# A stream of gated cross-attention layers: bias row as a TensorE product, norms shared, adds and setup moved

## The chip, the cores and the metric

The kernel runs on one core of one Trainium2 chip. The metric is the device time of one execution in microseconds (us), lower is better. A core has five engines that run their own instruction streams and meet at semaphores: TensorE (PE, with its weight loads PEld), VectorE (DVE), ScalarE (ACT), GpSimd (POOL) and SyncE (SP, which issues DMAs). All data is float32.

## What is computed

Four decoder layers work on x, 16 sequences of 256 rows and 128 features. Each adds a gated cross-attention over 64 context rows (16 heads of 8), then a gated feed-forward part; a layer norm precedes each.

```python
x = x + tanh(g_xattn[l]) * xattn_l(layernorm(x), ctx)   # softmax(q k' / sqrt(8) + bias_l) v, then @ Wo.T + bo
x = x + tanh(g_ffn[l])   * ffn_l(layernorm(x))
# ffn_0: 8 experts, 2 chosen a row, and a shared expert;  ffn_1: x @ (ternary weights).T
# ffn_2: 4 experts with fixed gates, relu;                ffn_3: 8 experts, 1 chosen a row
```

## The kernel before

The program has these stages on each engine, in this order: layer norm and attention of layer 0 (to about 249 us), the router's logits, ranks (`rank_tensor`, `route_vector`), the shared expert (`shared_*`), a setup, the experts of layer 0 (`moe_*`), then the **stream** (about 590 to 1141 us), and after it norm, routing and experts of layer 3.

The setup (`tern_prepare_vector`, `setup_tensor`, `setup_vector`) rounds the ternary weights and computes, for layers 1 to 3, the row `bvc @ Wo + bo` (value bias through the output projection, plus the output bias). `setup_tensor` makes that row on all 128 partitions of bank psM and begins with a wait for `s_tw`, which DVE's first instruction of `tern_prepare_vector` (L1166) raises. `setup_vector` multiplies it by the layer's gate into `bx` (L1193). DVE's order is `route_vector`, `shared_vector`, `tern_prepare_vector`, `setup_vector`, `moe_vector`; PE's is `rank_tensor`, `shared_tensor`, `setup_tensor`, `moe_tensor`.

The stream is a software pipeline over 48 batches (16 in each of the layers 1, 2, 3), written out by hand: step n, from -5 to 49, does for several batches one part each, in a fixed order on each engine.

- PE: turns probabilities (L1325, four times), queries of batch n+3 (L1301), values weighed (L1340, twice), heads turned (L1357), outputs turned (L1347), the transposes of a norm (`norm_rows`, L1294), an expert's first product (`four_up`, L1381), then keys, values (L1286), the ternary product (L1370) or the expert's second product (`four_down`, L1389), the projection of batch n-2 (L1363), and last the scores of batch n+3 (L1314).
- ACT: copies each of these out of PSUM (L1453, L1459, L1465, L1471, L1479), takes exponentials (L1475) and the experts' relus (L1486). The last two relus must end before the step's scores, which write the same banks.
- DVE: adds the mask bias (L1536, two tiles), row maxima (L1544, two tiles), between these the ternary result (`add_ternary`, L1574) or an expert's result (`add_four`, L1583) that PE made in the step before, scales the outputs of batch n-1 (L1549, L1553), and adds the projection of batch n-2 to x with row statistics (`add_attention`, L1561).
- POOL: subtracts the maxima (`shift`, L1620, two tiles), computes scale and shift of a norm from the statistics (`spread`, L1628 to L1638, seven small instructions), normalises 4 tiles of 128 rows (a chunk; L1647) and adds a bias row to x (`add_row`, L1654): `bx` after the norm for the queries, so that the attention's bias is already in x, and `b2c` after that for the experts of layer 2.

Query norms run at odd n on POOL and are transposed by PE at n+1; feed-forward norms run at even n and are transposed at n+1. One PSUM bank, psB, is shared: norm transposes, keys, values, the ternary product and the experts' second product fill it in turn. `take_bank` waits until its last user has read it (`s_free`); for the ternary and expert products that is DVE's add, one step later. The 16 first products of layer 2's experts lie on steps 22 to 29, 31 to 37 and 39 (`up_step`), each second product one step behind. Steps are counted in the text by their scores: those of step n are the last products that PE makes in it.

Of the kernel before, what the change touches and what calls it, by code (L numbers as in the profile page):

```python
# [21 lines left out]
P = 128  # L22
# [70 lines left out]
def build(nc, ins, out, sorted_x, sorted_y):  # L93
    ctx = ExitStack()
    with ctx:
# [19 lines left out]
        bx = sb("bx", [P, LAYERS - 1, D])  # L115
# [92 lines left out]
        lna = sb("lna", [P, CH, 2])  # L208
        lnd = sb("lnd", [P, CH])
        lnr = sb("lnr", [P, CH])  # L210
        lnh = sb("lnh", [P, CH])
# [36 lines left out]
        s_bx, s_b2 = sem("attention_bias_added"), sem("expert_bias_added")  # L248
# [978 lines left out]
        def values_at(n):  # L1227

            return {2: (2, 0), 3: (2, 1), 4: (2, 2), 5: (2, 3), 17: (3, 0), 19: (3, 1), 21: (3, 2), 22: (3, 3)}.get(n)
# [18 lines left out]
        for n in range(FIRST, FINAL):  # L1248
            for kind, c in (("query", query_norm(n - 1)), ("ffn", ffn_norm(n - 1))):
# [21 lines left out]
        def stream_tensor(pe):  # L1271
# [125 lines left out]
            for n in range(FIRST, FINAL):  # L1397
# [14 lines left out]
                if ffn_norm(n - 1) is not None:  # L1412
                    norm_rows(("ffn", ffn_norm(n - 1)))
# [21 lines left out]
        def stream_scalar(act):  # L1435
# [57 lines left out]
            for n in range(FIRST, FINAL):  # L1493
# [14 lines left out]
                if ffn_norm(n - 1) is not None:  # L1508
                    keep_normed(("ffn", ffn_norm(n - 1)))
# [17 lines left out]
        def stream_vector(dve):  # L1527
# [65 lines left out]
            for n in range(FIRST, FINAL):  # L1593
# [4 lines left out]
                if ternary_at(n - 1) is not None:  # L1598
                    add_ternary(ternary_at(n - 1))
                if down_at(n - 1) is not None:  # L1600
                    add_four(down_at(n - 1))
                if 0 <= 2 * n + 5 < NU:
                    row_max(2 * n + 5)
                if 0 <= n - 1 < NB:
                    scale_outputs(n - 1)
                if 0 <= n - 2 < NB:
                    add_attention(n - 2)

        def stream_gpsimd(pool):
# [12 lines left out]
            def spread(use):  # L1622

                c = use[1]
                if normed[use]:
                    pool.wait_ge(s_xn, normed[use])
                tiles = slice(c % NC * CH, c % NC * CH + CH)
                step(nc.gpsimd.tensor_tensor(lna[:], st[:, tiles, 1:3], st[:, tiles, 4:6], ALU.add))  # L1628
                step(nc.gpsimd.tensor_tensor(lnd[:], st[:, tiles, 1], st[:, tiles, 4], ALU.subtract))
                pool.wait_ge(s_lnp, steps[0])  # L1630
                step(nc.gpsimd.tensor_tensor(lna[:], lna[:], lnc[:].rearrange("p c -> p () c").broadcast_to([P, CH, 2]), ALU.mult))
                step(nc.gpsimd.tensor_tensor(lnd[:], lnd[:], lnd[:], ALU.mult))
                pool.wait_ge(s_lnp, steps[0])
                step(nc.gpsimd.tensor_scalar(lnd[:], lnd[:], 0.25, EPS, ALU.mult, ALU.add))
                pool.wait_ge(s_lnp, steps[0])
                step(nc.gpsimd.tensor_tensor(lnd[:], lnd[:], lna[:, :, 1], ALU.add))
                pool.wait_ge(s_lnp, steps[0])
                step(nc.gpsimd.tensor_tensor(lnr[:], lnd[:], lnh[:], ALU.pow))  # L1638

            def normalise(use):  # L1640
                kind, c = use
                m = normed[use]
                if m > 1:
                    pool.wait_ge(s_full, turn[[k for k in normed if normed[k] == m - 2][0]] + 1)
# [163 lines left out]
```

## Time and profile before

| | |
|---|---|
| median of 3 runs | 1357.03 us (1356.96 to 1357.54) |
| the profiled execution | 1357.12 us, its span 1355.2 us |
| busy over the span | PE 1055.8, DVE 781.6, ACT 659.0, POOL 698.0 us |
| stream, 623 to 728 us (105 us) | PE 91.6, DVE 77.6, ACT 73.7, POOL 92.3 us |
| stream, 728 to 820 us (92 us) | PE 78.7, DVE 68.6, ACT 64.4, POOL 82.7 us |
| stream, 820 to 940 us (120 us) | PE 103.1, DVE 56.9, ACT 66.9, POOL 69.0 us |
| stream, 940 to 1085 us (145 us) | PE 126.7, DVE 71.7, ACT 78.6, POOL 79.9 us |
| chain that ended last | PE 57%, DVE 13%, issue 11%, ACT 8%, POOL 7% |
| granted PE clock | 0.90 on the mean; 1.0 in most of the stream; 0.5 (1.2 GHz) at 280 to 292 us, 370 to 385 us and 1147 to 1184 us |

The profile gives for each instruction its engine, its line in the kernel, what it writes and reads, its start and duration, and what ended the idle time ahead of it. Busy time alone doesn't say what bounds a stage, since each engine also waits for the others inside a step. The timeline of a step shows that: who starts the moment that whose work ends.

### The profile page before, as it was taken

What the parts mean: (1) busy time and instruction counts of PE and PEld (TensorE: products, weight loads), DVE (VectorE), ACT (ScalarE), POOL (GpSimd) and SP (SyncE); (2) the same over time, 40 slices, a digit from 0 to 9 for tenths busy, and PEclk for the clock granted to TensorE, in tenths of its full rate; (3) what the DMA queues carried; (4) which work ended last, traced back from release to release, by engine and by line L of the source; (5) the groups of instructions that cost most, each with busy time, mean ns of one, the idle gap of its engine ahead of it and who ended that gap; (6) DMA issues with size and microseconds to landing.
All of it is one profiled execution on the core that took longest, in us unless ns stands there. A gap on an engine that the chain in (4) does not pass through costs nothing.

```text
span 1355.2 us, 26685 instructions
## 1 busy us (share of the span) xinstructions
PE 1055.8 (78%) x9100; PEld 852.9 (63%) x9100; DVE 781.6 (58%) x1697; ACT 659.0 (49%) x1372; POOL 698.0 (52%) x900
## 2 busy tenths in 40 slices
PE   0699999669979999547988889888888886508990
PEld 0477776446779999425766666666566664408990
DVE  3899998350076665555787775445544585234652
ACT  1544443333145666227767765545555565205650
POOL 0254454117781071676999897555654451055224
PEclk9799999669978999558999999999999998558995
DMA  8900000001121242100000000000400000002323
GB/s 252 285 6 1 1 1 1 1 4 47 61 69 47 77 114 73 51 19 1 2 1 1 2 2 1 1 1 2 140 1 1 1 2 1 0 31 90 89 72 93
DMA packets 75428, 55.81 MB, mean 41 GB/s; under 512 B 7363, under 2 KB 68419, under 8 KB 75204
## 3 DMA queue, kind: packets, MB, share of 16 engines
q1 hardware_dynamic: 69188, 41.92, 10.8%
q0 software_dynamic: 6144, 12.60, 3.1%
q8 instruction: 62, 1.02, 0.3%
q14 instruction: 34, 0.28, 0.1%
HBM read 32.48 MB, written 22.02 MB: 40 GB/s over the span
## 4 chain that ended last, share of the span: by engine, by line
PE 57%; DVE 13%; issue 11%; ACT 8%; POOL 7%; SPq 1%; DMA 1%; DVEq 1%; ACTq 0%; POOLq 0%
PE psS L966 9%; PE psO L972 8%; PE psO L1389 4%; PE psS L1381 4%; PE psS L1314 3%; PE psT L1325 3%; POOL xrows L1137 3%; PE psO L895 2%; PE psS L887 2%; PE psM L461 2%; PE psO L1340 2%; DVE rden L679 2%; DVE mx L1544 2%; ACT xrows L1486 2%; DVE ring L667 2%
## 5 line engine op out<-in xcount | busy, mean ns | idle before, releaser
L1620 POOL TENSOR_TENSOR ring<-ring,mx 128x1024 f32<-128x1024 f32 x96 | 182.3, 1903 | 145.8 <-DVE mx L1544 145.6
L1453 ACT ACTIVATE pT<-psT 128x512 f32<-128x512 f32 x192 | 114.8, 598 | 157.9 <-PE psT L1325 157.4
L1017 ACT ACTIVATE pT<-psS,b1copy 128x128 f32<-128x128 f32 x512 | 145.9, 368 | 87.4 <-PE psS L966 87.4
L1137 POOL DMA_INDIRECT xrows<-sorted_y,rows x96 | 92.4, 962 | 182.8 <-DMA sorted_y<-pT 95.1
L966 PE MATMUL psS<-ring 128*128 128x128 f32 x1024 | 140.4, 282 | 12.3 <-DVE ring L1040 11.6
L1536 DVE TENSOR_TENSOR ring<-psS,bias 128x1024 f32<-128x1024 f32 x96 | 113.1, 1220 | 61.9 <-PE psS L1314 61.8
L972 PE MATMUL psO<-ring,pT 128*128 128x128 f32 x1024 | 137.5, 278 | 0.7 <-ACT pT L1017 0.7
L966 PEld LDWEIGHTS psS<-ring 128*128 128x128 f32 x1024 | 129.4, 199 | 13.2 <-issue 7.9
L1325 PE MATMUL psT<-ident,ring 128*128 128x128 f32 x768 | 123.0, 283 | 15.0 <-ACT pT L1453 14.2
L741 POOL TENSOR_TENSOR ring<-ring,rden 128x1024 f32<-128x1024 f32 x32 | 75.3, 2354 | 114.6 <-DVE rden L681 114.6
L972 PEld LDWEIGHTS psO<-ring,pT 128*128 128x128 f32 x1024 | 126.8, 195 | 1.1 <-ACT pT L1017 1.1
L1325 PEld LDWEIGHTS psT<-ident,ring 128*128 128x128 f32 x768 | 86.0, 143 | 57.0 <-issue 34.5
L1037 DVE COPY ring<-w 128x512 f32 x128 | 60.2, 470 | 95.3 <-PE psO L972 73.5
L1544 DVE TENSOR_REDUCE mx<-ring 128x16 f32<-128x1024 f32 x96 | 114.0, 1208 | 0.0
L1125 POOL DMA_INDIRECT sorted_x<-late,ix x96 | 93.7, 976 | 37.0 <-issue 24.1
L1561 DVE SCALAR_TENSOR_TENSOR x<-psM,tg,x 128x256 f32<-128x256 f32 x48 | 23.2, 483 | 145.5 <-PE psM L1363 145.4
L1475 ACT ACTIVATE ring<-ring 128x1024 f32<-128x1024 f32 x96 | 101.5, 1059 | 0.0
L629 ACT ACTIVATE pT<-psT 128x512 f32<-128x512 f32 x64 | 38.2, 597 | 75.5 <-PE psT L545 75.5
L1647 POOL TENSOR_SCALAR xn<-x,lna,lnr 128x128 f32<-128x128 f32 x160 | 69.7, 450 | 0.2
L1294 PE MATMUL psO<-ident,xn 128*128 128x128 f32 x160 | 26.3, 290 | 55.7 <-POOL xn L1647 27.6
L679 DVE TENSOR_REDUCE rden<-ring 128x64 f32<-128x1024 f32 x32 | 61.4, 1917 | 0.0
L1389 PE MATMUL psO<-w,xrows 128*128 128x128 f32 x512 | 60.0, 276 | 1.5 <-ACT kblk L1479 0.8
(229 smaller groups left out, 2227.4 us busy)
## 6 DMA issues: line engine op xcount, KB each, us to landing
w<-w_dram SPq DMA_DIRECT2D x34, 256.0 KB, 6.0
ring<-sorted_x SPq DMA_DIRECT2D x32, 256.0 KB, 2.9
sorted_y<-pT SPq DMA_DIRECT2D x32, 256.0 KB, 2.3
sorted_x<-late SPq DMA_DIRECT2D x20, 256.0 KB, 3.5
out_dram<-x SPq DMA_DIRECT2D x1, 2048.0 KB, 8.7
sorted_x<-late,ix POOLq DMA_INDIRECT x96, 2.2
xrows<-sorted_y,rows POOLq DMA_INDIRECT x96
ctxz<-ctxz_dram SPq DMA_DIRECT2D x1, 1056.0 KB, 11.9
```

The source lines that it names most:

```text
L966: mm = nc.tensor.matmul(psS[:, t % 2, f * P:(f + 1) * P], wcopy[:, t, 0, f, :], xgT[:, s, t * P:(t + 1) * P], start=True, stop=True)
L972: mm = nc.tensor.matmul(psO[:, s, t * P:(t + 1) * P], hs[:, t % 2, f, :], wcopy[:, t, 1, f, :], start=(f == 0), stop=(f == nf - 1))
L1017: op = nc.scalar.activation(hs[:, t % 2, f, :], psS[:, t % 2, f * P:(f + 1) * P], func, bias=b1copy[:, t, f:f + 1])
L1125: nc.gpsimd.indirect_dma_start(sorted_x[h], bass.IndirectOffsetOnAxis(ix[:, s, m:m + 1], 0), xstage[:, s, m // nch, :], None).then_inc(s_s ...
L1137: nc.gpsimd.indirect_dma_start(fetched[:, at + m, :], None, sorted_y[c // (NC // 2)], bass.IndirectOffsetOnAxis(rows[:, c * nt + m:c * nt ...
L1325: mm = nc.tensor.transpose(psT[:, i * P:(i + 1) * P], ring[:, u % NS, p * P:(p + 1) * P], ident[:])
L1389: mm = nc.tensor.matmul(psB[:, t * P:(t + 1) * P], fourT[:, i % 2, k, t * P:(t + 1) * P], w22[:, e, f, :], start=(k == 0), stop=(k == 3))
L1453: nc.scalar.activation(pT[:, u % 2, 4 * h:4 * h + 4, :].rearrange("p a q -> p (a q)"), psT[:, :], ACT.Copy).then_inc(s_pT, 1)
L1475: nc.scalar.activation(ring[:, u % NS, :], ring[:, u % NS, :], ACT.Exp).then_inc(s_exp, 1)
L1536: nc.vector.tensor_tensor(ring[:, u % NS, :].rearrange("p (g h k) -> p g h k", g=NG, h=GH), psS[:, :, qt * 256:(qt + 1) * 256].rearrange(" ...
L1544: nc.vector.tensor_reduce(mx[:, u % 4, 0:NH], ring[:, u % NS, :].rearrange("p (h k) -> p h k", k=SK), AXX, ALU.max).then_inc(s_max, 1)
L1620: nc.gpsimd.tensor_tensor(rows_, rows_, mx[:, u % 4, 0:NH].rearrange("p h -> p h ()").broadcast_to([P, NH, SK]), ALU.subtract).then_inc(s_ ...
```

## The change

Five things are changed together.

1. The gate is left out of the bias row. `bx` is gone; `bo` holds the row for each layer, and PE adds it to the projection by a one-row product (ones times row) accumulated behind each of the two products of L1363. `add_row` is no longer called for the queries, and `add_attention` no longer waits for it.
2. The feed-forward norms run at odd n, with the query norms, and `spread` does the small instructions once for both, over two chunks. The feed-forward chunk is normalised one step later (even n) and transposed by PE at odd n; the ternary product moves from step 2c+6 to 2c+8.
3. `add_ternary` and `add_four` run on DVE in the step in which PE makes the product, after the outputs are scaled, not in the next step between the row maxima.
4. The experts' first products lie on steps 24 to 39 without a gap; one value product moves from step 22 to 23.
5. The setup runs ahead of the shared expert, on PE and on DVE.

```diff
-                nc.vector.tensor_scalar(bx[:, l - 1, :], psM[:, l * D:(l + 1) * D], tg[:, l:l + 1], None, ALU.mult).then_inc(s_four, 1)
+                nc.vector.tensor_copy(bo[:, l, :], psM[0:1, l * D:(l + 1) * D]).then_inc(s_four, 1)
...
         def ffn_norm(n):
-            return (n - 4) // 2 if n % 2 == 0 and 0 <= (n - 4) // 2 < 2 * B // 2 else None
+            return (n - 5) // 2 if n % 2 and 0 <= (n - 5) // 2 < 2 * B // 2 else None
...
         def ternary_at(n):
-            return (n - 6) // 2 if n % 2 == 0 and 0 <= (n - 6) // 2 < B // 2 else None
-        up_step = [22 + 17 * i // 15 for i in range(2 * NC)]
+            return (n - 8) // 2 if n % 2 == 0 and 0 <= (n - 8) // 2 < B // 2 else None
+        up_step = [24 + i for i in range(2 * NC)]
...
             def project(n):
                 pe.wait_ge(s_onT, n + 1)
                 for qt in range(QT):
-                    mm = nc.tensor.matmul(psY[:, qt * P:(qt + 1) * P], onT[:, qt * P:(qt + 1) * P], wat[:, layer(n), 3, :], start=True, stop=True)
+                    nc.tensor.matmul(psY[:, qt * P:(qt + 1) * P], onT[:, qt * P:(qt + 1) * P], wat[:, layer(n), 3, :], start=True, stop=False)
+                    mm = nc.tensor.matmul(psY[:, qt * P:(qt + 1) * P], ones1[:, :], bo[:, layer(n), :], start=False, stop=True)
                 mm.then_inc(s_y, 1)
...
-                if ffn_norm(n - 1) is not None:
-                    norm_rows(("ffn", ffn_norm(n - 1)))
+                if ffn_norm(n - 2) is not None:
+                    norm_rows(("ffn", ffn_norm(n - 2)))
...
                 dve.wait_ge(s_y, n + 1)
-                dve.wait_ge(s_bx, n // 2 + 1)
...
-                if ternary_at(n - 1) is not None:
-                    add_ternary(ternary_at(n - 1))
-                if down_at(n - 1) is not None:
-                    add_four(down_at(n - 1))
                 if 0 <= 2 * n + 5 < NU:
                     row_max(2 * n + 5)
                 if 0 <= n - 1 < NB:
                     scale_outputs(n - 1)
+                if ternary_at(n) is not None:
+                    add_ternary(ternary_at(n))
+                if down_at(n) is not None:
+                    add_four(down_at(n))
                 if 0 <= n - 2 < NB:
                     add_attention(n - 2)
...
-                cq, cf = query_norm(n), ffn_norm(n)
+                cq, cf, last = query_norm(n), ffn_norm(n), ffn_norm(n - 1)
...
-                    spread(("query", cq))
                 if cf is not None:
                     pool.wait_ge(s_bnf, CH * (cf + 1))
-                    spread(("ffn", cf))
+                if cq is not None or cf is not None:
+                    spread(cq, cf)
                 if 0 <= 2 * n + 5 < NU:
                     shift(2 * n + 5)
                 if cq is not None:
                     normalise(("query", cq))
-                    add_row(("query", cq), bx[:, layer(2 * cq) - 1, :], s_bx)
-                if cf is not None:
-                    normalise(("ffn", cf))
-                    if cf >= B // 2:
-                        add_row(("ffn", cf), b2c[:], s_b2)
+                if last is not None:
+                    normalise(("ffn", last))
+                    if last >= B // 2:
+                        add_row(("ffn", last), b2c[:], s_b2)
...
             rank_tensor(pe, 0)
+            setup_tensor(pe)
             shared_tensor(pe)
-            setup_tensor(pe)
...
             route_vector(dve, 0)
-            shared_vector(dve)
             tern_prepare_vector(dve)
             setup_vector(dve)
+            shared_vector(dve)
```

## Rows read from the trace of the kernel before

**Rows 1.** Waits of PE: who <- whom, us in all, times, longest us.

```profile
PE psO L1294 <- DVE x L1583: 17.1, 13, 1.3
...
PE psO L1294 <- DVE x L1574: 11.0, 8, 1.4
```

**Rows 2.** Timeline: start, duration (us), engine, line, tiles [idle <- releaser]; late steps.

```profile
1062.11 1.15 PE L1314 MATMUL psS<-xnT,qTs 32*128 32x256 f32 x16
...
1084.68 1.15 PE L1314 MATMUL psS<-xnT,qTs 32*128 32x256 f32 x16
...
1093.44 1.15 PE L1314 MATMUL psS<-xnT,qTs 32*128 32x256 f32 x16
...
1101.26 1.15 PE L1314 MATMUL psS<-xnT,qTs 32*128 32x256 f32 x16
...
1108.59 1.15 PE L1314 MATMUL psS<-xnT,qTs 32*128 32x256 f32 x16
```

**Rows 3.** Timeline: plain products, then the shared expert's with one-row products.

```profile
535.20 1.06 PE L966 MATMUL psS<-ring 128*128 128x128 f32 x8
...
536.09 1.05 PE L972 MATMUL psO<-ring,pT 128*128 128x128 f32 x8
...
311.08 1.16 PE L895 MATMUL psO<-w,ring 128*128 128x128 f32 x8
...
312.17 0.48 PE L896 MATMUL psO<-b,ones 1*128 1x128 f32 x2
...
312.58 1.16 PE L895 MATMUL psO<-w,ring 128*128 128x128 f32 x8
```

**Rows 4.** Timeline of PE in steps 26 and 27, with both expert products.

```profile
883.56 0.65 PE L1340 MATMUL psO<-pT,w 128*32 128x128 f32 x16
...
885.12 1.15 PE L1314 MATMUL psS<-w,qTs 32*128 32x256 f32 x16 [0.91 <-ACT xrows L1486]
...
888.58 0.65 PE L1347 MATMUL psO<-ident,oTs 128*128 128x128 f32 x4
890.55 0.63 PE L1294 MATMUL psO<-ident,xn 128*128 128x128 f32 x4 [1.31 <-DVE x L1583]
...
900.99 1.15 PE L1314 MATMUL psS<-w,qTs 32*128 32x256 f32 x16 [0.91 <-ACT xrows L1486]
```

**Rows 5.** Timeline of PE: scores of steps 1, 6, 7, 8, 16, 17, 21.

```profile
627.27 1.15 PE L1314 MATMUL psS<-xnT,qTs 32*128 32x256 f32 x16
...
672.78 1.15 PE L1314 MATMUL psS<-xnT,qTs 32*128 32x256 f32 x16
...
681.69 1.15 PE L1314 MATMUL psS<-xnT,qTs 32*128 32x256 f32 x16
...
690.02 1.15 PE L1314 MATMUL psS<-xnT,qTs 32*128 32x256 f32 x16
...
763.29 1.15 PE L1314 MATMUL psS<-w,qTs 32*128 32x256 f32 x16
...
773.50 1.15 PE L1314 MATMUL psS<-w,qTs 32*128 32x256 f32 x16
...
810.56 1.15 PE L1314 MATMUL psS<-w,qTs 32*128 32x256 f32 x16
```

**Rows 6.** Timeline around the shared expert and the setup.

```profile
291.53 8.88 PE L887 MATMUL psS<-xnT,w 128*128 128x512 f32 x16
...
302.45 0.19 DVE L857 TENSOR_TENSOR pw<-rs 128x32 f32<-128x32 f32 x1
...
369.02 0.75 DVE L935 SCALAR_TENSOR_TENSOR x<-psO,tg,x 128x512 f32 x1 [5.26 <-PE psO L896]
...
370.02 0.53 PE L1186 MATMUL psM<-wat,bvc 128*128 128x128 f32 x2 [1.16 <-DVE wab L1166]
...
374.54 1.09 PE L958 MATMUL psT<-ident,ring 128*128 128x128 f32 x4
...
383.17 3.75 PE L966 MATMUL psS<-ring 128*128 128x128 f32 x16 [7.54 <-DVE ring L1040]
```

More of the change, by code:

```diff
@@ L207, in build @@
         rc = sb("rc", [P, NH, 2])
[L208 to L211, printed above, removed]
+        lna = sb("lna", [P, 2, CH, 2])
+        lnd = sb("lnd", [P, 2, CH])
+        lnr = sb("lnr", [P, 2, CH])
+        lnh = sb("lnh", [P, 2, CH])
         bvs = rden[:].rearrange("p s k -> p (s k)")
@@ L1248, in build @@
         for n in range(FIRST, FINAL):
-            for kind, c in (("query", query_norm(n - 1)), ("ffn", ffn_norm(n - 1))):
+            for kind, c in (("query", query_norm(n - 1)), ("ffn", ffn_norm(n - 2))):
                 if c is not None:
@@ L1507, in stream_scalar @@
                     keep_normed(("query", query_norm(n - 1)))
-                if ffn_norm(n - 1) is not None:
-                    keep_normed(("ffn", ffn_norm(n - 1)))
+                if ffn_norm(n - 2) is not None:
+                    keep_normed(("ffn", ffn_norm(n - 2)))
                 if 0 <= n < NB:
@@ L1620, in shift, with spread @@
                 nc.gpsimd.tensor_tensor(rows_, rows_, mx[:, u % 4, 0:NH].rearrange("p h -> p h ()").broadcast_to([P, NH, SK]), ALU.subtract).then_inc(s_shift, 1)
[L1622 to L1629, printed above, removed]
+            def spread(cq, cf):
+                chunks = sorted(c % NC for c in (cq, cf) if c is not None)
+                k = len(chunks)
+                if cq is not None:
+                    first = normed["query", cq]
+                else:
+                    first = normed["ffn", cf]
+                if first:
+                    pool.wait_ge(s_xn, first)
+                pair = slice(chunks[0], chunks[-1] + 1, max(chunks[-1] - chunks[0], 1))
+                rows_ = st[:].rearrange("p (c t) s -> p c t s", c=NC)[:, pair]
+                a2, dd, rr = lna[:, 0:k], lnd[:, 0:k], lnr[:, 0:k]
+                step(nc.gpsimd.tensor_tensor(a2, rows_[:, :, :, 1:3], rows_[:, :, :, 4:6], ALU.add))
+                step(nc.gpsimd.tensor_tensor(dd, rows_[:, :, :, 1], rows_[:, :, :, 4], ALU.subtract))
@@ L1630, in spread @@
                 pool.wait_ge(s_lnp, steps[0])
-                step(nc.gpsimd.tensor_tensor(lna[:], lna[:], lnc[:].rearrange("p c -> p () c").broadcast_to([P, CH, 2]), ALU.mult))
-                step(nc.gpsimd.tensor_tensor(lnd[:], lnd[:], lnd[:], ALU.mult))
+                step(nc.gpsimd.tensor_tensor(a2, a2, lnc[:].rearrange("p c -> p () () c").broadcast_to([P, k, CH, 2]), ALU.mult))
+                step(nc.gpsimd.tensor_tensor(dd, dd, dd, ALU.mult))
                 pool.wait_ge(s_lnp, steps[0])
-                step(nc.gpsimd.tensor_scalar(lnd[:], lnd[:], 0.25, EPS, ALU.mult, ALU.add))
+                step(nc.gpsimd.tensor_scalar(dd, dd, 0.25, EPS, ALU.mult, ALU.add))
@@ L1635, in spread @@
                 pool.wait_ge(s_lnp, steps[0])
-                step(nc.gpsimd.tensor_tensor(lnd[:], lnd[:], lna[:, :, 1], ALU.add))
+                step(nc.gpsimd.tensor_tensor(dd, dd, a2[:, :, :, 1], ALU.add))
                 pool.wait_ge(s_lnp, steps[0])
-                step(nc.gpsimd.tensor_tensor(lnr[:], lnd[:], lnh[:], ALU.pow))
+                step(nc.gpsimd.tensor_tensor(rr, dd, lnh[:, 0:k], ALU.pow))
+                if cq is not None:
+                    place["query", cq] = chunks.index(cq % NC)
@@ L1640, in normalise @@
+                if cf is not None:
+                    place["ffn", cf] = chunks.index(cf % NC)
+            place = {}
             def normalise(use):
                 kind, c = use
-                m = normed[use]
+                m, k = normed[use], place[use]
                 if m > 1:
-                    pool.wait_ge(s_full, turn[[k for k in normed if normed[k] == m - 2][0]] + 1)
+                    pool.wait_ge(s_full, turn[[v for v in normed if normed[v] == m - 2][0]] + 1)
                 pool.wait_ge(s_lnp, steps[0])
```

7 lines of the change are left out of this document (3 added, 4 removed).

## The prediction

> **What bounds the kernel now.** Three views were read in this order: the waits of TensorE (PE) by stage, the timeline of single steps, and the timeline around the setup. The stream runs steps n = -5 to 49, and each step from -3 to 44 ends PE's part with the score products of L1314, so the distance between two L1314 starts is the length of a step. In the steps with expert work (22 to 40) PE waits 13 times, 17.1 us, ahead of the transposes of L1294 for VectorE's (DVE's) L1583, which has to free the shared bank psB; in the steps before, 8 times, 11.0 us, for L1574 [rows 1]. POOL is nearly full in those earlier steps (0.88 to 0.90 busy in the table's windows), yet it waits now and then for DVE's row maxima; PE is the engine that sets the pace. PE's order in a step is fixed, and inside it there is a second loop that no view names: PE turns probabilities, ACT keeps them, keeps the heads, takes an exponential, keeps the next probabilities, and only then PE turns the last quarter, projects, weighs values and makes scores. Step 43, with nothing else in it, has that loop alone: 7.33 us (1101.26 to 1108.59) [rows 2]. It contains the projection.
>
> **The bias as a product, on PE.** Per step 2 to 49 two one-row products (a float32 product is two records) stand behind the two projections of L1363. Plain products of 128 columns run at 8 records in 0.89 us (535.20 to 536.09), 0.22 us a product. In the shared expert's second layer four plain products and one one-row product take 1.50 us (311.08 to 312.58) [rows 3]. The insertion therefore costs 1.50 - 4 x 0.22 = 0.61 us, not 0.22: each change between 128 rows and one row leaves a gap. The second one stands ahead of the value products, where such a gap is already (they use 32 columns), so it costs what its own row takes from start to next start, 312.17 to 312.58, 0.41 us. That is **0.61 + 0.41 = 1.02 us a step**. Ends: 0.44 (two plain products) and 1.22 (twice 0.61); I take 1.02, the same instruction in the same place behind a product. In light steps everything after the projection moves by it.
>
> The Trainium skill, "TensorEngine Tiling (Array Packing)", Key Properties, says that changing the tiling mode drains TensorE, which speaks against this edit, and the rows agree (0.61 against 0.22). The same notes' "TensorE: Matmul & The Clock Gate", the table under Why this matters for your kernels, gives a product of few rows the time of one of 128; by that the edit would cost 0.44 us a step.
>
> In heavy steps (both expert products) PE starts the value products at 883.56, 0.65 long, and L1314 only at 885.12, after 0.91 us of idling for ACT's relus; as a product starts some 0.08 us ahead of the modelled end of the last, the cover is 0.99 of the 1.02, and **0.03 us a step** is left [rows 4]. If that cover were gone, 16 steps would pay 0.99 more each.
>
> **Adding the expert's or ternary result in its own step.** DVE's add moves from between the row maxima of the next step to behind the scaling of the outputs. There DVE is idle in heavy steps, and the bank is free long before PE's next L1294. The stall: L1347 starts at 888.58 and L1294 at 890.55, 1.97 us later, of which four records need some 0.5. So 1.47 us goes, and the step to 900.99, 15.87 long, becomes 14.40 [rows 4]. What queues behind the new wait on DVE is the attention add (L1561), which has to wait for PE's projection anyway, and that comes after the same product. Late next is the relu wait, already in the 14.40. In light odd steps less comes back, since ACT's loop is next: 8.91 (672.78 to 681.69) [rows 5] falls to 7.82, the length of step 42, which has a norm's transposes and no stall (1093.44 to 1101.26) [rows 2].
>
> **The norms of the feed-forward one step later, and one spread for two.** POOL does seven small operations once in two steps, not twice (2.46 us saved a pair), and drops 24 bias adds of 1.27 us, less what the power over twice the elements costs (0 to 1.0 us; the adds over 4 and 8 elements take 0.2 both, so I take 0). POOL is not what PE waits for, bar 0.8 us at step 4, and none of this shortens a step beyond that. If the power doubled, query rows would come up to 1 us late in steps 8, 10 and 12.
>
> **The sum of the stream**, steps from L1314 to L1314.
> - Steps 2 to 21 take 183.29 us now (627.27 to 810.56). After, with 1.02 in each: even with ternary, 8.33 (681.69 to 690.02) + 1.02 = 9.35; odd with a norm 7.82 + 1.02 = 8.84; odd without one 7.33 + 1.02 and its products. Steps 8, 10, 12, 18, 20: 5 x 9.35; 6, 7, 9, 11: 4 x 8.84; 17, 19, 21 with value products, 10.21 now (763.29 to 773.50), 1.0 less for the stall and 1.02 more, 3 x 10.23 [rows 5]. The rest are estimates: 13 to 16, where key products add 0.5 to a light step, 4 x 9.34; 2 to 5, as now with 1.02 each, less 0.5 in step 4 and 1.4 in step 5, whose norm moves away, 39.4 together. Sum 189.6: **+6.3**. It assumes that a slow clock seen around step 11 (about 1.6 us over two steps) doesn't recur.
> - Steps 22 to 41 take 282.88 (810.56 to 1093.44). After: 22 light with ternary, 9.35; 23 with values, 10.23; 24 with only the up product and 40 with only the down product, 22.57 + 0.43 + 1.02 = 24.0 (39 and 40 now take 22.57, 1062.11 to 1084.68; 24 has a norm's transposes more, 0.43, and a relu wait that hides the bias); 25 to 38 both, 14 x 14.43 = 202.0; 39 without a norm 14.0; 41 8.35. Sum 267.9: **-15.0** [rows 2, 5].
> - Steps 42 to 44: 3 x 1.02 = **+3.1**. Steps 45 to 49 have projections too and little cover (some 0.2 to 0.5 us of DVE work in two of them): **+4.4**.
> Stream: -1.2 us.
>
> **Setup ahead of the shared expert.** Now PE goes from the ranks straight into the shared expert (291.53) while DVE still routes until 302.64. Moved ahead, setup_tensor waits for L1166, which stands behind all of the routing: PE starts it at about 303.0, needs 4.5 us (370.02 to 374.54) and begins the shared expert at 307.5, 16.0 us later. The shared expert now begins at the low clock, 1.2 GHz, after PE's idling in the routing: its first 16 records take 8.88 us where 0.43 us each, as in its later groups, would make 7.1, a loss of 1.8 us; after the change part of that rise is spent on the setup's products, so I return 1.2: 14.8 us late. At the other end: now the last residual (369.02, 0.75 long) is followed by setup on PE and 6.6 us of setup on DVE, and the experts' first product starts at 383.17. After, the residual ends at 384.6, weights are copied (0.75 of register load and 1.0 of copies), transposes and their copy need as long, and the first product starts near 386.4: **+3.2 us** [rows 6]. From here to the stream PE, then POOL's gathers set the pace, so the shift stays. Ends: 0 and +5.
>
> **Total.** -1.2 + 3.2 = +2.0 us on the span of 1355.2, with 1.9 around it: 1359.1. The profiled execution took 1357.12, the median is 1357.03, so nothing is to be corrected. I predict 1359.1.
>
> **Rivals.**
> - *One-row products cost as plain ones.* Then some 31 light steps give back 0.58 us each, 18 us: 1341.1. For it: row counts don't change the columns streamed. Against: what the insertion takes in the shared expert [rows 3]. Chance 0.12.
> - *The cover in heavy steps fails (slower).* The relus of L1486 are released through the probabilities that PE turns ahead of the projection; if they ended later by what PE gained at L1294, the 1.02 us would show in 16 steps: +16, 1374.9. It decides from 0.99 us a step. Against: ACT's relus hang on a transpose that precedes the projection. Chance 0.10.
> - *The setup's move costs nothing*, because the DVE work that it takes from behind the shared expert weighs more or the clock stays high: 1355.9. Chance 0.10.
> - *The slow clock stays or comes more often in the light steps*: 1.6 us a time, 1360.7 to 1363.9. Seen once. Chance 0.12.
> - *The forecast*, 0.56, own range 1355 to 1363.
> A measurement of this kernel tells 0.2%, 2.7 us, from no change. The forecast's case gives 0.04 to faster, 0.28 to same, 0.24 to slower; with the rivals faster 0.20, same 0.36, slower 0.44. For 8 in 10 the range is 1350 to 1368; it leaves out the first rival and the second, and takes in bias prices of 0.74 to 1.22 us.
>
> **What would show it.** No wait of PE at L1294 for DVE; heavy steps of 14.4 us; odd light steps of 8.8 and steps 43 and 44 of 8.35 (7.8 if the products are cheap); 1.02 us more from L1363 to L1340; the shared expert starting near 307.5 and the experts near 386.4. Heavy steps over 15 us, or light ones under 8, would make it wrong.

## The result and the profile after

| | before | changed |
|---|---|---|
| median (8 executions each) | 1357.37 us (1354.91 to 1358.94) | 1366.41 us (1361.19 to 1373.58) |
| ratio | | 1.0071, 95% interval 1.0049 to 1.0094 |
| profiled execution, span | 1357.12, 1355.2 us | 1365.11, 1363.3 us |
| PE, DVE, ACT, POOL busy | 1055.8, 781.6, 659.0, 698.0 us | 1099.4, 784.8, 657.1, 643.4 us |

The changed kernel is 9 us slower. 1359.1 was forecast, 1350 to 1368 was the range: the measured time lies inside, on the side that was given the larger chance, but above the 1355 to 1363 of the forecast's own case, and the forecast had only 2.0 of the 8.1 us by which the span grew.

Line numbers of the changed kernel are one lower than those of the kernel before (the scores are L1313, the projection L1362, its one-row product L1363), on POOL up to 12 higher. First the heavy steps, where [rows 4] showed a stall at the norm's transposes and one at the scores. Timeline of PE, scores of step 26 to scores of step 27; columns as in [rows 2]:

```profile
884.84 1.15 PE L1313 MATMUL psS<-w,qTs 32*128 32x256 f32 x16
...
888.29 0.66 PE L1346 MATMUL psO<-ident,oTs 128*128 128x128 f32 x4
888.79 0.60 PE L1293 MATMUL psO<-ident,xn 128*128 128x128 f32 x4
...
898.25 0.48 PE L1363 MATMUL psM<-bo,ones 1*128 1x128 f32 x2
898.67 0.65 PE L1339 MATMUL psO<-pT,w 128*32 128x128 f32 x16
899.24 1.13 PE L1313 MATMUL psS<-w,qTs 32*128 32x256 f32 x14
```

L1293 starts 0.50 us after L1346, without idling, and no wait of PE for DVE's adds is left in the stream (28.1 us in [rows 1]). The idling for ACT's relus ahead of the scores is gone too: the one-row products fill it. The step is 14.40 us long.

A light step with nothing else in it is step 43 (scores at 1100.95 for step 42, at 1109.30 for step 43: 8.35 us, where [rows 2] had 7.33):

```profile
1100.95 1.15 PE L1313 MATMUL psS<-xnT,qTs 32*128 32x256 f32 x16
...
1107.17 0.39 PE L1362 MATMUL psM<-wat,attnT 128*128 128x128 f32 x2
1107.48 0.48 PE L1363 MATMUL psM<-bo,ones 1*128 1x128 f32 x2
1107.90 0.49 PE L1362 MATMUL psM<-wat,attnT 128*128 128x128 f32 x2
1108.32 0.48 PE L1363 MATMUL psM<-bo,ones 1*128 1x128 f32 x2
1108.73 0.65 PE L1339 MATMUL psO<-pT,late 128*32 128x128 f32 x16
1109.30 1.15 PE L1313 MATMUL psS<-xnT,qTs 32*128 32x256 f32 x16
```

From the projection to the value products it is 1.56 us, against 0.54 before: 1.02 us, to the hundredth what [rows 3] gave. The same place in the kernel before:

```profile
1107.47 0.61 PE L1363 MATMUL psM<-wat,attnT 128*128 128x128 f32 x4
1108.01 0.65 PE L1340 MATMUL psO<-pT,late 128*32 128x128 f32 x16
```

What the forecast's sum left out is a half-rate clock inside the stream. Timeline around the scores of step 11, then busy time and granted clock of three stretches (columns: window, length, PE busy, granted clock, DMA share, GB/s):

```profile
723.14 0.66 PE L1324 MATMUL psT<-ident,ring 128*128 128x128 f32 x4 [1.22 <-ACT pT L1453]
...
724.37 0.49 PE L1362 MATMUL psM<-wat,attnT 128*128 128x128 f32 x2
724.79 0.75 PE L1363 MATMUL psM<-bo,ones 1*128 1x128 f32 x2
725.47 1.08 PE L1339 MATMUL psO<-pT,late 128*32 128x128 f32 x16
726.48 2.09 PE L1313 MATMUL psS<-xnT,qTs 32*128 32x256 f32 x16
```

```profile
724.90:731.80 6.90, 6.90 (x58) 0.51 0.01 2
1117.80:1121.00 3.20, 3.20 (x28) 0.53 0.02 5
1146.20:1149.20 3.00, 2.96 (x8) 0.50 0.00 0
```

Most such stretches are found without the clock's view: the 16 records of the scores take 2.09 us at half rate (1.2 GHz) and 1.15 at full rate (2.4 GHz). One that ends between two scores is missed (e4 has one). The kernel before had one behind step 1, from 715.1 to 718.5 us, at the scores of step 11. The first steps of the stream run at half rate in every profile (up to 619.5 us in that of the kernel before), which the table of the time before doesn't list.

### The profile page after: what moved, and what is told of

The parts are those of the page before. It is cut to its first block, busy times and chain, and to the rows that moved or that the text cites. A ratio compares the mean times of both kernels' runs of the same rounds, so it can differ in the third digit from the quotient of the medians.

```text
span 1363.3 us, 26870 instructions
## 1 busy us (share of the span) xinstructions
PE 1099.4 (81%) x9292; PEld 880.9 (65%) x9292; DVE 784.8 (58%) x1697; ACT 657.1 (48%) x1372; POOL 643.4 (47%) x764
## 4 chain that ended last, share of the span: by engine, by line
PE 64%; DVE 10%; issue 8%; POOL 7%; ACT 7%; SPq 1%; DMA 1%; DVEq 1%; ACTq 0%; POOLq 0%
PE psS L965 8%; PE psO L971 8%; PE psT L1324 5%; PE psO L1389 4%; PE psS L1381 4%; PE psO L1339 4%; PE psS L1313 3%; POOL xrows L1136 3%; PE psM L1363 3%; PE psO L894 2%; PE psS L886 2%; PE psM L460 2%; PE psM L1362 2%; DVE rden L678 2%; DVE ring L666 2%
## 5 line engine op out<-in xcount | busy, mean ns | idle before, releaser
L1582 DVE TENSOR_TENSOR x<-psO,x 128x512 f32<-128x512 f32 x16 | 11.1, 691 | 85.1 <-PE psO L1389 85.1
```

## Where the 8.1 us lie

Both spans, cut at the same instructions:

| part | forecast | measured | what makes the difference |
|---|---|---|---|
| up to the stream's first scores | +3.2 | +4.8 | 596.02 became 600.82 |
| steps -2 to 1 | 0 | -0.3 | |
| steps 2 to 21 | +6.3 | +9.4 | half clock in steps 11 and 12: 2.9 us; steps 8, 10, 12 of 9.55, not 9.35 |
| steps 22 to 41 | -15.0 | -15.3 | |
| steps 42 to 44 | +3.1 | +3.3 | |
| steps 45 to 49 | +4.4 | +7.5 | half clock: 1.6 us from 1117.84 on (against e2, which has the same steps), 1.3 in the last projection |
| layer 3 | 0 | -1.4 | the half clock at its experts' start ends earlier |

The last projection shows what the half clock does to the new products: 0.73 us from start to start for each pair of records, and the projection takes 2.96 us with them, where it takes 1.63 at full clock (1107.17 to 1108.80) and the kernel before needed 0.71. The first row is that of before:

```profile
1139.04 0.71 PE L1363 MATMUL psM<-wat,attnT 128*128 128x128 f32 x4 [0.47 <-ACT attnT L1471]
```

```profile
1146.22 0.79 PE L1362 MATMUL psM<-wat,attnT 128*128 128x128 f32 x2 [0.47 <-ACT attnT L1471]
1146.95 0.79 PE L1363 MATMUL psM<-bo,ones 1*128 1x128 f32 x2
1147.67 0.80 PE L1362 MATMUL psM<-wat,attnT 128*128 128x128 f32 x2
1148.39 0.79 PE L1363 MATMUL psM<-bo,ones 1*128 1x128 f32 x2
```

## The experiments

Twelve kernels ran in four groups, each group on a chip of its own beside the kernel before. On three of the four chips the kernel before took 1459 to 1469 us. The 100 us more lie in the shared expert and the experts of layers 0 and 3, where engines stand still for over 30 us at a time; the profile puts these waits down to "remote", a releaser outside what it shows, and the profiles of the faster chips have no such wait. The shared expert took 102 to 122 us there, here 77. The stream is the same there to 0.1 us a step. So ratios are compared on one chip, and the stream, from its first scores to the first product of the norm behind it, is compared across chips. Lengths of steps in us, from scores to scores (* holds half clock behind step 1; the stream's first steps hold it in all):

| kernel | step 9 | 10 | 18 | 26 | 43 | 2 to 21 | 22 to 41 | stream |
|---|---|---|---|---|---|---|---|---|
| before | 8.91 | 8.33 | 8.32 | 15.87 | 7.33 | 183.3* | 282.9 | 548.9* |
| changed | 8.84 | 9.55 | 9.36 | 14.41 | 8.35 | 192.7* | 267.6 | 553.5* |
| e1, bias on POOL | 7.82 | 9.54 | 8.33 | 14.37 | 7.33 | 176.0 | 263.3 | 522.8 |
| e2, setup back | 8.84 | 9.55 | 9.35 | 14.41 | 8.35 | 189.8 | 267.6 | 548.6* |
| e3, moves only | 7.81 | 9.57 | 8.33 | 14.37 | 7.33 | 176.1 | 263.3 | 522.8 |
| e4, 128 rows | 8.26 | 9.55 | 8.77 | 14.37 | 7.78 | 183.0* | 264.7 | 534.2* |
| e5, changed again | 8.84 | 9.55 | 9.35 | 14.41 | 9.62* | 192.5* | 267.8* | 557.5* |
| e6, setup only | 9.84* | 8.96* | 8.34 | 15.88 | 7.32 | 183.3* | 282.9 | 548.9* |
| e7, bias only | 9.93 | 9.35 | 9.35 | 15.92 | 10.75* | 205.5* | 287.0* | 589.9* |
| e8, neighbours | 8.65 | 9.56 | 9.16 | 14.37 | 8.88* | 188.2* | 266.2 | 547.9* |
| e9, adds only | 8.73 | 8.38 | 8.33 | 14.37 | 7.33 | 176.6 | 263.5 | 523.7 |
| e10, power split | 7.82 | 8.93 | 8.34 | 14.37 | 7.53* | 173.3 | 262.9 | 522.0* |
| e11, norm first | 7.82 | 8.33 | 8.33 | 14.37 | 7.33 | 171.3 | 262.9 | 515.0 |
| e12, 128 rows, setup back | 8.26 | 9.55 | 8.78 | 14.37 | 7.77 | 181.7 | 264.7 | 532.8 |

### e1, bias back on POOL

```diff
-                    nc.tensor.matmul(psY[:, qt * P:(qt + 1) * P], onT[:, qt * P:(qt + 1) * P], wat[:, layer(n), 3, :], start=True, stop=False)
-                    mm = nc.tensor.matmul(psY[:, qt * P:(qt + 1) * P], ones1[:, :], bo[:, layer(n), :], start=False, stop=True)
+                    mm = nc.tensor.matmul(psY[:, qt * P:(qt + 1) * P], onT[:, qt * P:(qt + 1) * P], wat[:, layer(n), 3, :], start=True, stop=True)
...
                     normalise(("query", cq))
+                    add_row(("query", cq), bx[:, layer(2 * cq) - 1, :], s_bx)
```

> The changed kernel, but the bias row is added by POOL as before; the other four edits stay. Theory A (the bias products cost 1.02 us in every step without relu cover, and nothing in steps 24 to 39): 26 light steps of the stream give back 1.02 each (26.5), the steps 45 to 49 give back about 4.9, so 1366.4 - 31.4 = 1335 us; odd light steps with a norm 7.8 us, even ternary steps 8.3, heavy steps unchanged at 14.4 with an idle time of PE of about 1 us for ACT's relus at L1313. Theory B (POOL is the bound of the light steps as soon as PE is lighter, since it now has 1.27 us more to do in two steps): pairs of light steps of 16.6 us instead of 16.15, and 1339 us. Theory C (the one-row products cost like plain ones, the rest of the miss is the clock): 1366.4 - 26 x 0.44 - 2 = 1353 us.

1430.28 us beside 1459.34, ratio 0.9795 (0.978 to 0.9811); e2, which has the products, took 1458.83 on the same chip: 28.6 us less. Steps 9, 18 and 43 give back 1.02 us each, step 26 gives back 0.04. But steps 8, 10 and 12 give back nothing: 9.55 us with the products and without. So theory A holds with a hole in it, and the pairs of light steps are 17.4 us long, longer than B's. Something else than the bias had made the even steps longer.

### e2, setup back

```diff
-            setup_tensor(pe)
             shared_tensor(pe)
+            setup_tensor(pe)
...
-            tern_prepare_vector(dve)
-            setup_vector(dve)
             shared_vector(dve)
+            tern_prepare_vector(dve)
+            setup_vector(dve)
```

> The changed kernel, but the setup stands behind the shared expert again, on PE and DVE. Theory A (the 4.8 us by which the stream starts later come from this edit and nothing gives them back): 1366.4 - 4.8 = 1361.6 us, the shared expert starting at 291.5 us and the experts' first product near 383.2. Theory B (my sum, 3.2 us): 1363.2 us. Theory C (the setup's move costs nothing in the end, since the clock's low stretches shift with it): 1366 us.

1458.83 us, ratio 0.9992 (0.9979 to 1.0005). The changed kernel itself did not run on this chip, so e2 alone doesn't price the setup; e1 and e3 differ in it alone (1430.28 and 1428.60 us), 1.7 us, less than their intervals tell apart. e2's worth is another: no score product behind step -3 ran at half clock, and its stream took 548.6 us, the kernel before's 548.9. The kernel before has one half-clock stretch, worth 1.6 us, in its 548.9; e2 has half clock in its last projection alone (2.96 us, 1.3 of it the clock's). At full clock, then, both streams take some 547.3 us: the stream's four edits together cost and gain nothing there.

### e3, the moves inside the stream only

The edits of e1 and e2 together.

> Only the edits inside the stream (norms at odd steps with one spread, adds in their own step, expert products on steps 24 to 39); bias on POOL and setup behind the shared expert as in the kernel before. Theory A: 1335 - 4.8 = 1330 us, faster than both kernels: 15 us from the heavy steps, 1.1 us from each odd light step with a norm. Theory B (POOL as the bound): 1334 us. Rival (the heavy steps' 15 us were gained only because the bias products sat in the relu wait; without them the wait comes back in full and nothing changes, or the scatter of the clock eats the gain): over 1340 us.

1428.60 us, ratio 0.9793 (0.9778 to 0.9808): faster than the kernel before by 2.1%, and the rival falls. Steps 22 to 41 take 19.6 us less, odd steps 1.1 us less, but the even steps of 9.57 show where gain is missing. Timeline of POOL and PE in step 12 (in steps 8 and 10 the wait is 1.52 and 1.50 us):

```profile
794.29 1.65 POOL L1645 TENSOR_TENSOR lnr<-lnd,lnh 128x8 f32<-128x8 f32 x1
795.90 1.91 POOL L1620 TENSOR_TENSOR ring<-ring,mx 128x1024 f32<-128x1024 f32 x1
797.79 1.75 POOL L1660 TENSOR_SCALAR xn<-x,lna,lnr 128x128 f32<-128x128 f32 x4
799.59 0.65 PE L1294 MATMUL psO<-ident,xn 128*128 128x128 f32 x4 [1.50 <-POOL xn L1660]
```

PE idles for 1.50 us at the norm's transposes, now for POOL. The chain is: power, subtraction of the second tile's maxima, normalising, transposes. The power stands in it with 1.65 us.

### e4, a bias product of 128 rows

```diff
-                nc.vector.tensor_copy(bo[:, l, :], psM[0:1, l * D:(l + 1) * D]).then_inc(s_four, 1)
+                nc.vector.tensor_scalar(bx[:, l - 1, :], psM[:, l * D:(l + 1) * D], 1.0 / P, None, ALU.mult).then_inc(s_four, 1)
...
-                    mm = nc.tensor.matmul(psY[:, qt * P:(qt + 1) * P], ones1[:, :], bo[:, layer(n), :], start=False, stop=True)
+                    mm = nc.tensor.matmul(psY[:, qt * P:(qt + 1) * P], onesm[:, :], bx[:, layer(n) - 1, :], start=False, stop=True)
```

> The changed kernel, but the bias product has 128 rows (ones 128 x 128 times a matrix whose 128 rows are the bias row over 128) instead of one, so TensorE multiplies more and computes the same. Theory A (each change between 128 rows and one row leaves a gap; two more plain products cost 0.44 us a step, 0.58 less than now): 26 x 0.58 + 2.3 = 17.4 us less, 1349 us; from L1362 to L1339 0.98 us instead of 1.55. Rival (a second product onto the same bank costs what it costs, whatever its rows): 1366 us, 1.55 us from L1362 to L1339.

1438.99 us, ratio 0.9862 (0.9844 to 0.9881), 19.8 us less than e2, of which 14.4 lie in the stream; the rest lies outside it and isn't explained (the two kernels differ in the place of the setup too). Timeline of PE in step 43:

```profile
1168.24 0.39 PE L1363 MATMUL psM<-wat,attnT 128*128 128x128 f32 x2
1168.46 0.39 PE L1364 MATMUL psM<-bx,onesm 128*128 128x128 f32 x2
1168.68 0.39 PE L1363 MATMUL psM<-wat,attnT 128*128 128x128 f32 x2
1168.91 0.39 PE L1364 MATMUL psM<-bx,onesm 128*128 128x128 f32 x2
1169.22 0.65 PE L1340 MATMUL psO<-pT,late 128*32 128x128 f32 x16
```

0.98 us from projection to value products, as theory A said. With 128 times the multiplications the two products cost 0.44 us a step, not 1.02. Step 6 took 10.43 us, where e12 has 8.99 for it: a stretch at half clock lies in it, between two scores (columns as above):

```profile
749.70:753.10 3.40, 3.40 (x31) 0.50 0.00 0
```

### e5, the changed kernel again

No edit.

> The changed kernel itself, as the control for the three beside it, and to see whether the slow spells of the granted clock inside the stream lie where they lay before. Theory A (they are set by the program): again one in steps 11 and 12 and one at step 44, step 12 longer than 11 us. Theory B (they come and go from one execution to the next): steps 8, 10, 12 all 9.55 us, or a spell elsewhere. Time: 0.7% over the kernel before where the stages ahead of the stream behave as in the pages shown, the same as before within 0.2% where the layer 0 experts are held up by their own stalls.

1471.28 us beside 1462.34, ratio 1.0047 (1.0025 to 1.007), so the result stands on another chip. The stretches at half clock are not fixed: this profile has one at the scores of steps 7 and 11 and a row of them at the end, each 2.09 us long where 1.15 is the full clock's:

```profile
1173.29 2.09 PE L1313 MATMUL psS<-xnT,qTs 32*128 32x256 f32 x16
...
1183.86 2.09 PE L1313 MATMUL psS<-xnT,qTs 32*128 32x256 f32 x16
...
1193.48 2.09 PE L1313 MATMUL psS<-xnT,qTs 32*128 32x256 f32 x16
```

Its stream took 557.5 us, e2's with the same steps 548.6: the clock alone makes 8.9 us. Both theories are half right: the places recur (in all profiles that have such stretches they lie in steps 6 to 12 or from 41 on), how many of them fall differs from one execution to the next.

### e6, the setup alone

The edit of e2 the other way round, in the kernel before.

> The kernel before with nothing changed but the setup, which stands ahead of the shared expert on PE and DVE. Theory A (the move costs what the two pages show, 16 us later into the shared expert, 0.9 us from residual to transposes behind it, a stream 4.8 us later): ratio 1.0035, some 4.8 us more. Theory B (my sum): 3.2 us more. Theory C (where the stages ahead of the stream are held up by stalls of 20 us, the shift is swallowed): 0 within 2 us, with the stream starting at the same time as with the setup behind.

1466.78 us, ratio 1.0029 (1.0008 to 1.0049): 4.4 us more, with 1.2 and 7.2 us as ends. It costs something; whether it is A's 4.8 or the forecast's 3.2 can't be told. The profiles of this chip don't help: its stream started at 684.29 us, that of e7 with the setup behind at 681.63, those of e5 and e8 with the setup ahead at 681.69 and 681.48.

### e7, the bias alone

The edit of e1 the other way round, in the kernel before.

> The kernel before with nothing changed but the bias: one-row products on PE, no bias addition on POOL. Theory A (1.02 us in each step without relu cover, none in the 14 to 16 heavy steps, whose wait for ACT's relus of 0.91 us takes it up): steps 2 to 21 +18 to +20 us, steps 24 to 39 under +3, the rest +10; ratio 1.021, some 30 us more. Rival (the cover in the heavy steps fails without the moved adds): heavy steps 16.9 us instead of 15.87, some 44 us more. Rival (POOL was the bound of the light steps and the relief pays for the product): 10 us more.

1501.84 us, ratio 1.0257 (1.022 to 1.0294): by the ratio 38 us more, 8 above theory A. Heavy steps are 15.92 us: the relu wait covers all but 0.04 of 1.02 us without the moved adds as well, so that rival falls, and so does POOL's relief. Where nothing covers it the price is 1.02 (steps 9, 10, 18). The rest is the clock: steps 7, 8, 11, 12, 42 and 43 are 0.9 to 2.4 us longer than those of the kernel before at full clock (8.91 and 8.33 for 11 and 12) plus 1.02, and scores ran at half clock in steps 7, 11, 41, 42 and 44.

### e8, one-row products as neighbours

```diff
...
+                    if qt == 0:
                         nc.tensor.matmul(at, o, wat[:, layer(n), 3, :], start=True, stop=False)
                         mm = nc.tensor.matmul(at, ones1[:, :], bo[:, layer(n), :], start=False, stop=True)
+                    else:
+                        nc.tensor.matmul(at, ones1[:, :], bo[:, layer(n), :], start=True, stop=False)
+                        mm = nc.tensor.matmul(at, o, wat[:, layer(n), 3, :], start=False, stop=True)
```

> The changed kernel with the order of the four products of a projection changed: plain, one-row, one-row, plain instead of plain, one-row, plain, one-row. Same number and sizes of products, two changes of the row count fewer inside the group. Theory A (the price is the change of the row count, not the product): from the first L1362 to L1339 1.25 us instead of 1.56, light steps 0.31 us shorter, ratio to the changed kernel 0.993 (9 us less over 31 steps at most). Rival (a one-row product costs 0.41 us wherever it stands): no change, 1.56 us.

1462.56 us, ratio 1.0003 (0.9979 to 1.0026), 8.7 us less than e5 beside it. Timeline of PE in step 41:

```profile
1165.22 0.39 PE L1364 MATMUL psM<-wat,attnT 128*128 128x128 f32 x2
1165.54 0.48 PE L1365 MATMUL psM<-bo,ones 1*128 1x128 f32 x2
1165.87 0.38 PE L1367 MATMUL psM<-bo,ones 1*128 1x128 f32 x2
1166.18 0.49 PE L1368 MATMUL psM<-wat,attnT 128*128 128x128 f32 x2
1166.60 0.64 PE L1339 MATMUL psO<-pT,late 128*32 128x128 f32 x16
```

1.38 us: between A (1.25) and its rival (1.56). From start to next start the four products take 0.32, 0.33, 0.31 and 0.42 us; in the changed kernel (rows of step 43 above) it is 0.31, 0.42, 0.42, 0.41, and in e4 0.22, 0.22, 0.23, 0.31. One sum gives them all: 0.22 us a product, whatever its rows, and 0.10 us more on each side on which its neighbour is of another kind. The passage to the value products, which use 32 columns, counts as such a change, since the last product of e4 pays for it too. The one-row product has no price of its own: a product of 128 rows between two one-row products takes 0.42 us (1107.90 to 1108.32), as long as a one-row product between two of 128 rows. So A names the right cause and miscounts: the new order has one change fewer inside the group (two, not three), and the one ahead of the value products stays. It saves 0.18 us, so a change costs 0.2 us, half of it on either side. In 31 steps that is 5.6 of the 8.7 us; the streams of the two profiles differ in the clock too (10.2 us of half clock here, 23.9 in e5).

### e9, the adds alone

```diff
                 if 0 <= n - 1 < NB:
                     scale_outputs(n - 1)
+                if ternary_at(n) is not None:
+                    add_ternary(ternary_at(n))
+                if down_at(n) is not None:
+                    add_four(down_at(n))
```

with the calls for n - 1 ahead of the row maxima left out, in the kernel before.

> The kernel before with one edit: the ternary result's and the experts' adds run on DVE in their own step, behind the scaling of the outputs. Norms, spread, expert steps, bias and setup as before. Theory A (POOL sets the pace of the light steps 6 to 12, as it has 17 us to do in two steps there, and PE's stall at L1294 in them was slack): heavy steps 14.4 instead of 15.87 us, steps 17, 19, 21 1.1 us shorter, but pairs of the steps 6 to 12 stay at 17.2 us; some 24 us less than the kernel before. Theory B (my prediction's reading, PE's stall sets the odd light steps): pairs of 16.15 us in steps 6 to 16 as well, some 30 us less.

1442.00 us, ratio 0.9822 (0.9799 to 0.9844), 27 us less. Heavy steps are 14.37 us: this edit alone gives all that the heavy steps gain. In the light steps with norms A is right from step 8 on, where two steps take 17.1 us (8.73 + 8.38); step 7 was shortened to 7.87. PE's wait has changed its owner. In steps 7, 8 and 9:

```profile
765.14 0.66 PE L1294 MATMUL psO<-ident,xn 128*128 128x128 f32 x4 [0.31 <-POOL xn L1647]
...
773.46 0.66 PE L1294 MATMUL psO<-ident,xn 128*128 128x128 f32 x4 [0.76 <-POOL xn L1647]
...
782.70 0.66 PE L1294 MATMUL psO<-ident,xn 128*128 128x128 f32 x4 [1.17 <-POOL xn L1647]
```

After that it is 1.18 us in odd steps and 0.32 in even ones. POOL is busy 33.3 of the 35 us from 777 to 812. With the norms as before, POOL holds the light steps as soon as DVE doesn't.

### e10, the power split

e3 with the power done for the query's 4 values at once and for the other 4 behind the normalising.

```diff
-                step(nc.gpsimd.tensor_tensor(rr, dd, lnh[:, 0:k], ALU.pow))
+                step(nc.gpsimd.tensor_tensor(rr[:, own], dd[:, own], lnh[:, own], ALU.pow))
```

> The kernel with the moves inside the stream only (bias on POOL, setup behind the shared expert), with the power over 8 elements a partition split in two over 4 each, the query's first and the other behind the query's normalising. Theory A (in even steps 8 to 16 PE waits at L1294 for POOL's normalised rows, and the power of 1.65 us against 1.01 for half the elements stands in that chain): even steps 8, 10, 12 8.9 us instead of 9.57, 14 and 16 8.7 instead of 9.3, some 3 us less in all, ratio 0.977. Rival (POOL's total work is the bound, so that 0.37 us more of it costs what it costs): no gain, or 1 us more.

1439.59 us, ratio 0.9808 (0.9784 to 0.9832). Even steps 8, 10, 12 are 8.93 us instead of 9.57, as A said: the power stood in PE's chain. Steps 14 and 16 stay at 9.29, against A. They take 9.29 in the kernel before too, and here PE has no wait at L1294 in them, so POOL's chain isn't what holds them.

### e11, the norm first

e10 with the query's normalising ahead of the second subtraction.

```diff
+                if cq is not None:
+                    normalise(("query", cq))
                 if 0 <= 2 * n + 5 < NU:
                     shift(2 * n + 5)
-                if cq is not None:
-                    normalise(("query", cq))
```

> As the power split, and the query's rows are normalised ahead of the second subtraction of the step on POOL, so that PE gets them 1.9 us earlier and ACT gets the rows for its exponential 1.75 us later. Theory A (the chain over POOL to L1294 is what the even norm steps wait for): even steps 8, 10, 12 8.3 us, the wait of PE at L1294 for POOL gone, 3 us less than the power split. Rival (the exponential is then what comes late): PE waits at L1325 for ACT instead, in the even steps or the odd ones, and the pair stays or grows to 17.4 us.

1431.87 us, ratio 0.9754 (0.9731 to 0.9778), the best of all and 2.5% faster than the kernel before. Pairs of light steps are 16.15 us, and PE no longer idles at the transposes:

```profile
796.51 1.02 POOL L1646 TENSOR_TENSOR lnr<-lnd,lnh 128x4 f32<-128x4 f32 x1
797.71 1.73 POOL L1664 TENSOR_SCALAR xn<-x,lna,lnr 128x128 f32<-128x128 f32 x4 [0.18 <-POOL lnr L1646]
799.40 1.91 POOL L1620 TENSOR_TENSOR ring<-ring,mx 128x1024 f32<-128x1024 f32 x1
...
800.26 0.60 PE L1294 MATMUL psO<-ident,xn 128*128 128x128 f32 x4
```

The stream takes 515.0 us, 34 less than before. The later row for ACT's exponential costs nothing.

### e12, 128 rows again, on a chip like the first

The edits of e4 and e2 together.

> The changed kernel with the bias products of 128 rows and the setup behind the shared expert. What it tells apart is the granted clock: in the profiles so far the kernels with one-row products hold 15 score products at half clock in steps 0 to 44 in five profiles (steps 7 to 11 and 41 to 44), those without 3 in eight. Theory A (the gaps that one-row products leave bring the low clock): with as many products, but of 128 rows, no score product at half clock or one, and a ratio near 0.983 to 0.986. Rival (the chip brings it, since one chip gave most of them, or more products of any kind do): again two or more score products at half clock where the chip is another than the one of the 128-row run before, and a ratio nearer to 0.99.

1342.02 us beside 1357.10, ratio 0.9886 (0.9869 to 0.9902), on a chip where the kernel before takes what it took on the first. No score product behind step -1 ran at half clock, and its four executions lie within 1.2 us (1341.49 to 1342.70), where the eight of the changed kernel lay within 12.4. It is 24 us faster than the changed kernel on such a chip, from which it differs in the place of the setup too. Of the clock it shows what theory A expects, but e4, with the same products, had its one stretch in step 6. Of the ratio the rival's end holds: 0.9886 is near 0.99 and off A's 0.983 to 0.986. The clock need not be the reason: the stream is 16.1 us shorter than the kernel before's (548.9 to 532.8), of which the whole shows 15.1, and e4, whose ratio A was built on, has 5 us of its 20.3 outside the stream. Those were not followed.

## Why the prediction was right, and where it was short

- *The price of the bias product* (1.02 us a step): right, and for its reason. 1.02 in every step without cover (e1, e7), with the one-row form's extra 0.58 us gone in e4. The forecast took the price from the shared expert's rows as gaps at the changes, and e8 shows that it is nothing else: two products of 0.22 us and three more changes of 0.2 us. The Trainium skill, "TensorEngine Tiling (Array Packing)", Key Properties, says that a change of the tiling mode drains TensorE; that direction agrees with e8's 0.2 us a change. The Trainium skill's "TensorE: Matmul & The Clock Gate", the table under Why this matters for your kernels, gives few rows the time of 128; by that the price would be 0.44. The trace agrees for the product alone (0.22 us with either row count); what it adds is the price of the changes around it.
- *The cover in heavy steps*: right. 14.41 us measured, 14.43 forecast; 0.04 us a step left, 0.03 forecast. The rival that it fails is gone (e7: 15.92).
- *The adds in their own step*: right. e9 has it alone. What had to be seen was that [rows 4] gives 1.97 us between two starts of which 0.5 is work.
- *Even light steps*: near the number, and by luck, since the reason was wrong. The forecast was 8.33 + 1.02 = 9.35, measured 9.55, 9.35 without norms (step 18). In steps 8, 10 and 12 the bias adds nothing (e1); the merged norm had already made them 9.55. The step that failed is "so I take 0" for the power over twice the elements: it went from 1.01 to 1.65 us, in the middle of the range named there, and it isn't on POOL's sum that it hurts but in the chain to PE's transposes. That "none of this shortens a step" held; that it lengthens one was left as an if. By POOL's lines in the changed kernel, 620 to 830 us (name, shape, count, busy, mean ns, idle):

```profile
L1644 POOL TENSOR_TENSOR lnr<-lnd,lnh 128x8 f32<-128x8 f32 x9 | 14.8, 1647 | 0.7
L1644 POOL TENSOR_TENSOR lnr<-lnd,lnh 128x4 f32<-128x4 f32 x2 | 2.0, 1009 | 0.2
L1634 POOL TENSOR_TENSOR lna<-st 128x16 f32<-128x16 f32 x9 | 1.9, 216 | 0.0
```

- *The setup*: right in direction, 3.2 forecast, 4.8 in the profile. Two terms were off. The shared expert started at 307.47 us, as forecast, but got none of the 1.2 us back that the clock was to return: its first 16 records took 9.28 us, where they took 8.88 before, and its last residual ended at 386.12, not 384.6. And the experts' first product began 2.31 us behind the end of that residual, where I had 1.8:

```profile
307.47 9.28 PE L886 MATMUL psS<-xnT,w 128*128 128x512 f32 x16
...
385.37 0.75 DVE L934 SCALAR_TENSOR_TENSOR x<-psO,tg,x 128x512 f32 x1 [5.25 <-PE psO L895]
386.22 0.63 PE L957 MATMUL psT<-ident,ring 128*128 128x128 f32 x4 [1.01 <-issue]
...
388.43 2.34 PE L965 MATMUL psS<-ring 128*128 128x128 f32 x16 [1.58 <-DVE ring L1039]
```

- *The clock*: the largest miss. That the slow clock "doesn't recur" was the weak step; the rival put it at 1.6 us a time, with a chance of 0.12. In the profile it cost 2.9 + 1.6 + 1.3 us in the stream, and 8.9 us in e5. The profiles of the five kernels with one-row products hold 15 score products at half clock in steps 0 to 44, those of the nine others 3. By the granted clock itself, between step 1 and the last projection, the five hold 10.2, 0, 23.9, 27.3 and 10.2 us of half clock (the changed kernel, e2, e5, e7, e8); of the nine others four hold 3.4 us each (before, e4, e6, e10) and five none. e12 lacks it on a chip like the first, and e5, e7 and e8 have it on the chip on which e6 has 3.4 us, so the chip alone doesn't make it. Nor does a long pause of PE: in the 15 us ahead of each of thirteen such stretches (before, changed, e4, e5, e7) PE never idled for over 1.4 us at once. But each kernel has one profile only (the changed one two), the one-row products come with longer steps and other gaps, e2 has none, and no run changed the gaps alone: that one-row products bring the low clock is likely, and how is open.

With these terms the sum is 1359.1 + 1.6 (setup) + 5.8 (clock) + 0.6 (power) - 1.4 (layer 3) = 1365.7, beside 1365.11 in the profiled execution. The terms were read from that same profile, so this shows that nothing large is left out, and no more.

## What to carry to other kernels

Work that is moved from an engine that isn't the bound to the one that is costs its full length in every step whose cover is used up; here 18 of some 50 steps had cover (e7), most of them heavy ones. If a row has to be added on TensorE among products of 128 rows, give it 128 rows too: the two products cost 0.44 us a step, not 1.02, and the few executions measured scattered less. When an idle time goes, ask not only which engine is late next by its sum, but which chain ends at the same instruction: here the stall at the transposes went from DVE to POOL, and taking the power apart and moving the normalising up on POOL (e3 to e11) was worth 7.8 us of the stream.

## What the hardware showed that was not expected

- A power on POOL over 128 x 8 elements takes 1.65 us, over 128 x 4 1.01, while additions take 0.2 us over 4 to 16: four more elements a partition cost 0.64 us.
- A one-row product costs what one of 128 rows costs, 0.22 us from start to start (128 columns, float32). Each change between the two kinds costs 0.2 us more, half of it in the product ahead and half in the one behind. The sum fits the five groups seen: 0.54 us (kernel before), 0.98 (e4), 1.38 (e8) and 1.56 (changed), and the shared expert's 1.50.
- The same program takes 1357 us on some chips and 1459 to 1469 on others, with equal steps in the stream; the difference lies in the shared expert and the experts of layers 0 and 3, in waits of over 30 us whose releaser the profile doesn't show. The cause is open.
